# Second attention of a two-layer block: sine products and sums of the rotated queries and keys one slot later in the written order

## The reference, cut to what matters

```
q, k, v = xn @ Wq.T, xn @ Wk.T, xn @ Wv.T      # 32 heads of 64, float32
q = q*cos + rotate_half(q)*sin                 # the same for k
heads 0..29: blocks of 128 queries against 192 keys (64 before the block), causal
heads 30,31: all 1024 keys, causal
out = concat(softmax(q k / 8) v) @ Wo.T + bo
x = x + out * g                                # g from the gate network, computed earlier
```

## Time and profile before

| | us |
|---|---|
| median of 3 runs | 3315.84 (3314.36 to 3317.30) |
| the profiled execution | 3312.25 |
| its span, first to last instruction | 3310.5 |
| busy in the span: TensorE | 3110.0 |
| VectorE | 2337.0 |
| ScalarE | 1920.1 |
| GpSimd | 1144.1 |

### The profile page before, as it was taken

One profiled execution on the slowest core, in us unless ns is written; L12 is line 12 of the kernel. 1 busy time (PEld: TensorE's weight loads), 2 busy tenths in 40 slices (PEclk: granted clock), 3 DMA queues, 4 the chain that ended last, 5 costly groups with the idle time before them and its releaser, 6 DMA issues. The chain is left out here.

```text
span 3310.5 us, 62712 instructions
## 1 busy us (share of the span) xinstructions
PE 3110.0 (94%) x21586; PEld 2208.9 (67%) x21586; DVE 2337.0 (71%) x6577; ACT 1920.1 (58%) x4806; POOL 1144.1 (35%) x1689
## 2 busy tenths in 40 slices
PE   7999999979999999996988999999999999999998
PEld 5888888822333333323877888778877788778886
DVE  5777766559888888875656666776667766676665
ACT  4666666627767667673445555455555555455552
POOL 1111111010000010102016666466665666556663
PEclk9999999979999999998999999999999999999999
DMA  4111111042123132102224343343434444244432
GB/s 137 44 39 44 39 44 39 12 83 44 47 45 67 27 71 44 27 8 86 101 85 110 88 98 89 105 112 91 96 95 100 101 94 95 71 104 96 98 86 58
DMA packets 310383, 241.71 MB, mean 73 GB/s; under 512 B 150769, under 2 KB 256689, under 8 KB 309937
## 3 DMA queue, kind: packets, MB, share of 16 engines
q1 hardware_dynamic: 310064, 237.69, 29.1%
HBM read 100.71 MB, written 39.85 MB: 42 GB/s over the span
## 5 line engine op out<-in xcount | busy, mean ns | idle before, releaser
L1651 ACT ACTIVATE b_pp<-b_pp,b_nm 128x192 f32<-128x192 f32 (+2 forms) x1024 | 473.5, 465 | 573.2 <-DVE b_nm L1824 490.8
L903 DVE TENSOR_REDUCE a_mx<-ps 128x1 f32<-128x512 f32 x1024 | 636.9, 682 | 86.8 <-PE ps L851 86.7
L825 ACT ACTIVATE a_pt<-ps 128x512 f32<-128x512 f32 x1024 | 534.8, 601 | 244.0 <-PE ps L862 242.5
L1614 POOL TENSOR_SCALAR b_pp<-b_pp,b_rc 128x192 f32<-128x192 f32 x960 | 432.3, 472 | 231.0 <-DVE b_rc L1833 231.0
L1601 POOL TENSOR_TENSOR b_rt<-b_rt,b_sin 128x512 f32<-128x512 f32 x256 | 342.3, 1337 | 284.2 <-DMA b_rt<-b_qf 284.2
L851 PE MATMUL ps<-a_k,a_q 96*128 96x512 bf16 x1024 | 399.0, 391 | 19.3 <-DMA a_k<-qk_parts 16.4
L862 PE MATMUL ps<-a_q,a_k 99*128 99x512 bf16 x1024 | 386.9, 382 | 8.9 <-issue 5.4
L638 DVE SCALAR_TENSOR_TENSOR f_yac<-ps,f_cw,f_yac 128x128 f32<-128x128 f32 x992 | 277.0, 344 | 121.9 <-PE ps L447 120.4
L1845 DVE COPY b_pt<-ps 128x384 f32<-128x384 f32 (+3 forms) x456 | 246.9, 552 | 131.6 <-PE ps L1740 119.4
L1824 DVE CUSTOM_DVE_ANT_0 b_pp<-ps,b_mk 128x192 f32<-128x192 f32 x960 | 273.8, 350 | 34.8 <-PE ps L1719 33.9
L1774 PE MATMUL ps<-b_wo,b_oT 128*128 128x256 f32 x1024 | 249.0, 387 | 50.3 <-DVE b_pt L1845 45.8
(11 more groups left out here) (255 smaller groups left out, 7186.9 us busy)
## 6 DMA issues: line engine op xcount, KB each, us to landing
b_rt<-b_qf SPq DMA_DIRECT2D x1024, 64.0 KB, 2.0
qk_parts<-f_aa SPq DMA_DIRECT2D x32, 384.0 KB, 2.6
a_q<-qk_parts SPq DMA_DIRECT2D x192, 64.0 KB, 3.0
a_k<-qk_parts SPq DMA_DIRECT2D x96, 128.0 KB, 5.2
v_rows<-f_va_ SPq DMA_DIRECT2D x16, 512.0 KB, 3.0
a_v<-v_rows SPq DMA_DIRECT2D x4, 2048.0 KB, 11.7
b_raw<-in_W1qT SPq DMA_DIRECT2D x64, 128.0 KB, 2.7
b_raw<-in_W1kT SPq DMA_DIRECT2D x64, 128.0 KB, 3.0
```

Of the source, the lines that this page charges most:

```text
L825: e.activation(pt[(4 * i + j) % 8][:, :], P.ap(s), ACT.Exp).then_inc(P.free_sem(s), 1)
L903: e.tensor_reduce(mx[kh % 3][:, j * 4 + t, h:h + 1], P.ap(s), AX.X, ALU.max, negate=True).then_inc(P.free_sem(s), 1)
L1614: m = e.tensor_scalar(x, x, r[:, 2 * u + h:2 * u + h + 1], 1.0, ALU.mult, ALU.mult)
L1651: e.activation(x, x, ACT.Exp, bias=nm[n % 4][:, c:c + 1], scale=-1.0, accum_out=sm[n % 4][:, c:c + 1]).then_inc(exp_done, 1)
```

## The change

In `work(n)`, the sine product of part i moves from slot 2i + 2 to slot 2i + 3, and the sum from 2i + 3 to 2i + 4. Slots of 8 and above go to the next turn's slots 0, 1 and now 2, ahead of that turn's own steps. Projection and cosine product stay in slots 2i and 2i + 2.

```diff
-        out, rest = [[] for _ in range(8)], [[], []]
+        out, rest = [[] for _ in range(8)], [[] for _ in range(3)]
...
             parts = [("q", 0), ("k", 0), ("q", 1), ("k", 1)]
             for i, (x, half) in enumerate(parts):
                 of = (n + 1, int(x == "k"), half)
-                for slot, s in ((2 * i, "proj"), (2 * i + 2, "cos"), (2 * i + 2, "sin"), (2 * i + 3, "add")):
+                for slot, s in ((2 * i, "proj"), (2 * i + 2, "cos"), (2 * i + 3, "sin"), (2 * i + 4, "add")):
                     (out[slot] if slot < 8 else rest[slot - 8]).append((s, *of))
```

## The result

| | before | changed kernel |
|---|---|---|
| median of 4 runs each | 3316.57 us (3314.36 to 3319.96) | 3385.91 us (3381.82 to 3388.07) |
| ratio, 95% interval | | 1.0207 [1.0189, 1.0224] |
| profiled execution | 3312.25, span 3310.5 | 3381.82, span 3380.0 |
| mean granted clock | 0.983 | 0.977 |

The change made the kernel slower, by 69 us; 3360 had been predicted, with 3296 to 3404 as its range.

What follows compares the result with a forecast made beforehand. TensorE was taken as the bound, its output sums waiting 45.8 us for VectorE copies. Over 44 turns 0.60 + 1.32 - 0.82 gave +48 us, less 3: 3315.84 + 45, rounded to 3360 us, range 3296 to 3404.

Steps and rivals of the forecast that it cites:

- Step 1: Query sums' old place, between copies 2 and 3: VectorE's sine wait goes; second stride's reciprocal comes 0.90 us earlier.
- Step 2: Next stride, behind the score reductions: sine product delays the key's cosine product and copy 0; key projection waits 0.60 us.
- sign of being wrong: VectorE's key cosine products of 0.7 us, or key projections that start as before, would show the forecast wrong.
- forecast's pattern: Behind the reductions: query sum 0.69 us, GpSimd's sine product waiting for it, then key cosine products of about 1.8 us.
- Step 3: Second stride, two weight differences behind the sine product: same pattern, wait between 0.60 and 2.03 us, taken at 1.32.
- Step 4: Output sums' old wait for copy 2 goes: 0.82 us a turn.
- Rival 3: Second stride: both weight differences always go before the cosine product, 2.03 us; +77 us, 3393 us; chance 0.13.
- Rival 2: Both strides: cosine product always next behind the sine product, 0.60 us each; +17 less 3, 3330 us; chance 0.17.
- Rival 1: Cosine product follows the query sum without the sine between, copy 0 on time; about -38 us, 3278 us; chance 0.15.

Runs made afterwards that it cites:

- experiment 1: Kernel before with only the sine products one slot later, query sums left in their old slot: 3316.48 us, ratio 1.0001.
- experiments 5 to 7: Query sums alone moved, against the kernel before: 3320.70 us; changed kernel plus a small GpSimd instruction: 3299.55 us; query sums alone, run again: 3296.79 us.
- experiment 7: Unchanged reruns on one chip: query sums alone moved one slot later against the kernel before, median 3296.79 us; changed kernel, 3378.15 to 3294.52 us.
- near twin: Kernel before with the query sums alone one slot later, sine products left where they were: 3320.70 us, ratio 1.0025.

## Why the prediction was right, and where not

**Step 1, where the sums leave,** held: no sine wait is left there, and the second stride's reciprocal came early; it stands at 1871.72, 1871.72 - 1869.45 = 2.27 us after its output, where 2.37 was forecast:
```profile
1869.45 1.89 PE L1774 MATMUL ps<-b_wo,b_oT 128*128 128x256 f32 x8
...
1871.72 0.19 DVE L1833 RECIPROCAL b_rc<-b_sm 128x8 f32<-128x8 f32 x1
```
**Step 2, where they arrive,** had the place right, and the size nearly (0.47 us in first strides for 0.60), but by the wrong product; that the size fits is luck. It let the sum keep "the same length (0.69)" and made the sine product wait, as it had waited for the cosine product at 1912.82. But that row is itself a tie, 0.10 us between the starts, and so are the other 20 such meetings of the kernel before, at 98 to 107 ns, all won by VectorE. Nothing hung on the tie there: in experiment 1, which has the same order on VectorE, the offsets lay at 84 to 95 ns, the sine went first in 19 of 20 meetings, and the time was the same. These meetings have one product ahead of copy 0 and no differences behind the sine; with two products the tie decides the kernel. In the profiled execution of the result the sum lost every time. So the prediction's own sign of being wrong came up, key cosine products of 0.68 us, though not for the rival that it was tied to. The forecast's pattern, sum 0.69, sine 1.74, cosine some 1.8, exists, in experiments 5 to 7; there it costs only 0.35 us a stride (28.0 / 80).

**Step 3** was mis-sized: 1.32 us taken for the second stride, 1.85 measured, near the bound of 2.03, because the differences go ahead of the waiting product in every second stride where the sine does. Over the stage little of this is left: with 39 waits of 0.47 and 38 of 1.85, where 44 of each were forecast, the new waits came to 88.6 us for 44 x (0.60 + 1.32) = 84.5.

**Step 4** mostly held: 45.8 - 13.4 = 32 of the output sums' 46 us went.

**A term was missing:** TensorE's clock. The forecast sums waits alone and leaves TensorE's busy time as it was, without a reason. Its waits came out well, partly by errors of both signs: the idle time grew by 41.7 us for the 45 forecast. The 27.8 us of longer busy time, most of it from the stretches at 1.2 GHz behind long waits, are what the forecast was short of (26 us against the measured median).

**Rivals.** Rival 3, both differences always first, is what all three traces of the changed kernel show, at 3386 where it gave 3393. Rival 2, the cosine next behind the sine, is the pattern of the query sums alone in experiment 7; its 3330 was too high, as its 0.60 a stride was 0.35: 3297 was measured. TensorE's idle time there is 3295.2 - 3115.7 = 179.5 us, 21 less than before. Of these the two groups of waits make 45.8 - 28.0 - 10.6 = 7, and the smaller waits that shrank in the changed kernel some 10 more. Rival 2's condition was put at the wrong place: not what follows a sine that has won, but whether the sum or the sine wins. Rival 1's sign, a faster kernel, is then not excluded for this kernel either; 3 of 13 executions were faster than the kernel before.

The Trainium skill, "SBUF — State Buffer", section "Who interferes with whom", says that a VectorE instruction with two SBUF inputs contends with a GpSimd instruction that reads SBUF, and that issue order decides who blocks. The traces agree that one of the two waits until the other has ended (sums of 1.92 and 3.31 us beside sine products of 1.29). By recorded starts VectorE's product is ahead in all these meetings, and still lost 510 times of 512 below 94 ns; at this distance the order of the recorded starts is not what decides.

**Open:** what moves the offset by 10 to 20 ns from program to program and, by the times, from execution to execution; and why both differences go ahead of a product that has waited through the sine, when a waiting GpSimd instruction gets in after a single VectorE product.

## What to carry to other kernels

Before two products that share a resource are put side by side, look at how far apart they start: where a few tens of nanoseconds decide who waits, forecast both outcomes, and arrange the order so that either one is hidden (here: one product, not two, ahead of the copy that TensorE waits for, and the long GpSimd work away from it). That version was 2% faster than the kernel before and kept its time whichever way the tie fell. Time such a kernel on more than one chip and in many executions before believing a sign.

## What was not expected of the hardware

- A 0.11 us GpSimd instruction made the kernel 86 us faster (3385.91 to 3299.55), and a 0.06 us VectorE instruction made its near twin some 62 us slower (3320.70 to 3382.55).
- A VectorE product that lost to a sine product with two weight differences right behind it lost to these as well: 3.31 us for a 0.69 us product.
- Waits of TensorE of 1.85 us were followed, in 14 of 38 cases, by a spell at 1.2 GHz, worth 1.6 us each.
- One unchanged kernel ran at 3378 and at 3295 us on the same chip; the first belongs, by its trace, to one side of a tie at some 95 ns, the second, by its time, to the other.
